# Slot one-hots of two of each four tiles made by ScalarE in the fill of the bucket lists

## What is computed

```python
edge_index = jnp.stack([src, dst])
x = _layernorm(x + _L0_gnn_ref(x, edge_index, ...), axis=-1)
x = _layernorm(x + _L1_gnn_ref(x, src, dst, ...), axis=-1)
x = _layernorm(x + _L2_gnn_ref(x, edge_index, edge_weight1, ...), axis=-1)
x = _layernorm(x + _L3_gnn_ref(x, edge_index, edge_weight, ...), axis=-1)
```

## Time and profile before

| | us |
|---|---|
| median of 3 runs | 10,757.82 |
| lowest and highest | 10,753.19, 10,758.09 |
| the profiled execution | 10,751.21 |
| its span in the trace | 10,749.4 |
| busy in the span: TensorE, VectorE | 8389.9 (78%), 8209.4 (76%) |
| busy in the span: ScalarE, GpSimd | 4510.4 (42%), 1386.4 (13%) |

### The profile page before, as it was taken

One profiled execution on the slowest core, in us unless ns is written; L12 is line 12 of the kernel. 1 busy time (PEld: TensorE's weight loads), 2 busy tenths in 40 slices (PEclk: granted clock), 3 DMA queues, 4 the chain that ended last, 5 costly groups with the idle time before them and its releaser, 6 DMA issues. The chain is left out here.

```text
span 10749.4 us, 313973 instructions
## 1 busy us (share of the span) xinstructions
PE 8389.9 (78%) x96214; PEld 6815.6 (63%) x96215; DVE 8209.4 (76%) x16705; ACT 4510.4 (42%) x9074; POOL 1386.4 (13%) x1678
## 2 busy tenths in 40 slices
PE   2244668885888755899995999798999959769996
PEld 0232225664777644899994666444999936468896
DVE  4797777777999866666666999777888777788887
ACT  0120001113666411565654444586777746423333
POOL 0110001110000000466662000000000012100000
PEclk7555555556999855999997999899999979889998
DMA  2000000001444311333331888686455400000000
GB/s 49 4 0 13 4 4 11 12 12 47 162 161 161 124 36 36 109 122 125 122 125 58 273 275 274 227 291 210 143 144 145 139 12 5 4 4 3 3 3 13
DMA packets 618663, 984.99 MB, mean 92 GB/s; under 512 B 133030, under 2 KB 278381, under 8 KB 618586
## 3 DMA queue, kind: packets, MB, share of 16 engines
q1 hardware_dynamic: 487514, 810.18, 23.8%
q10 hardware_dynamic: 121152, 162.43, 4.2%
q0 software_dynamic: 9920, 11.51, 0.4%
HBM read 788.66 MB, written 195.21 MB: 92 GB/s over the span
## 5 line engine op out<-in xcount | busy, mean ns | idle before, releaser
L2523 POOL TENSOR_TENSOR acc<-acc,m_sum 128x544 f32<-128x544 f32 (+1 forms) x637 | 810.3, 1272 | 1229.4 <-ACT m_sum L2490 1189.1
L2387 DVE TENSOR_TENSOR m_msg<-m_vps,m_msg 128x512 f32<-128x512 f32 (+1 forms) x637 | 427.3, 671 | 414.5 <-PE m_vps L2428 376.7
L2452 PE MATMUL m_sps<-m_msg,m_oh 128*128 128x136 f32 x4900 | 697.9, 286 | 0.0
L2859 PE MATMUL u_sps<-u_r,u_oh 128*128 128x129 f32 x4900 | 657.0, 276 | 28.7 <-ACT u_r L2815 28.7
L1495 PE MATMUL sp_out_x<-x,sp_adj_x 128*128 128x128 f32 x4802 | 671.6, 284 | 0.0
L1479 PE MATMUL sp_aps_x<-sp_ohw_x,sp_oh_x 128*128 128x128 bf16 x7350 | 536.6, 221 | 166.5 <-DVE sp_ohw_x L1446 166.4
L2092 PE MATMUL s_qps<-q_parts,s_oht 128*128 128x128 bf16 x7203 | 511.5, 220 | 197.9 <-DVE s_oht L1562 146.3
L1508 ACT COPY sp_adj_x<-sp_aps_x 128x512 f32<-128x512 f32 (+1 forms) x637 | 362.4, 569 | 722.6 <-PE sp_aps_x L1479 722.6
L2843 PE MATMUL u_zps<-fcs,u_a 128*128 128x128 f32 x4916 | 654.7, 276 | 6.9 <-ACT u_a L2808 6.9
L2859 PEld LDWEIGHTS u_sps<-u_r,u_oh 128*128 128x128 f32 x4900 | 598.5, 192 | 37.7 <-issue 37.6
L2452 PEld LDWEIGHTS m_sps<-m_msg,m_oh 128*128 128x128 f32 x4900 | 610.5, 191 | 0.0
(11 more groups left out here) (595 smaller groups left out, 20318.6 us busy)
## 6 DMA issues: line engine op xcount, KB each, us to landing
u_e<-e_tiles SPq DMA_DIRECT2D x591, 256.0 KB, 2.8
e_tiles<-t_es ACTq DMA_DIRECT2D x588, 256.0 KB, 4.1
g_e<-e_tiles SPq DMA_DIRECT2D x588, 256.0 KB, 4.5
s_rows<-bucket_rows SPq DMA_DIRECT2D x148, 768.0 KB, 4.0
m_rows<-bucket_rows SPq DMA_DIRECT2D x148, 768.0 KB, 4.0
t_rows<-bucket_rows SPq DMA_DIRECT2D x148, 384.0 KB, 5.0
s_rows<-bucket_rows SPq DMA_DIRECT2D x49, 896.0 KB, 5.0
m_rows<-bucket_rows SPq DMA_DIRECT2D x49, 896.0 KB, 5.0
```

Source lines behind the costliest of these rows:

```text
L2452: last = nc.tensor.matmul(sps[x][:, at:at + M], oh[x][:, j * P:(j + 1) * P], msg[x][:, j * M:(j + 1) * M], start=True, stop=True)
L2523: nc.gpsimd.tensor_tensor(at, at, sums[x][:, 0:n * M], ALU.add).then_inc(added, 1)
L2859: last = nc.tensor.matmul(sps[:, :], oh[x][:, j * P:(j + 1) * P], zr[x][:, j * D1:(j + 1) * D1], start=(q == 0 and j == 0), stop=(q == las ...
```

## The change

Of each four tiles, VectorE makes the slot one-hots of the first two only (`bf_put` shrinks from 512 to 256 columns). ScalarE makes those of the other two: for each of the two tiles a Square of (iota - slot), with the negated slot as the bias column (`bf_minus`), into `bf_far` (128 x 256, one buffer), and one Relu of (1 - `bf_far`) over both tiles into `bf_aput` (two halves). Slots are integers, so the Relu gives 1 where they agree and 0 elsewhere. ScalarE gets the inner loop and the two table reads for each window, ahead of its copy of `bf_acc`. Two semaphores are new: `bf_far_made` (ScalarE waits for its own Squares) and `bf_act_made` (Relu is done: TensorE waits for it with each group, and so does ScalarE before the next Squares). Relu also waits for `filled`. The four matmuls stay; the third and fourth read their weights from `bf_aput`. `bf_minus` is made once, at the start of the stage, by one VectorE pass over all slots.

```diff
--- before.py
+++ after.py
@@ -1262,7 +1262,9 @@
         sb, ps, sem = scope(nc, ctx, k)
         col, cur, cur_iota = sb("bf_col", 1), sb("bf_cur", NT), sb("bf_iota", s.NB)
         oht = sb("bf_oht", 2 * NT * G, BF16)
-        put, spread_ = sb("bf_put", 2 * G * P, BF16), sb("bf_spread", 2 * FQ * NT * G, BF16)
+        put, aput, far, minus = sb("bf_put", 2 * 2 * P, BF16), sb("bf_aput", 2 * 2 * P, BF16), sb("bf_far", 2 * P, BF16), sb("bf_minus", z.NGS * G)
+        spread_ = sb("bf_spread", 2 * FQ * NT * G, BF16)
+        far_made, act_made = sem("bf_far_made"), sem("bf_act_made")
         zero_b = sb("bf_zero", FQ * NT, BF16)
         acc = ps("bf_acc", FQ * NT)
         lst = sb("bf_lst", FQ * NT, BF16)
@@ -1285,7 +1287,8 @@
                 nw = B.windows(dve, s)
                 nc.vector.memset(zero_b[:, :], 0.0).then_inc(ready, 1)
                 nc.vector.tensor_copy(cur_iota[:, :], k["iota_f"][:, 0:s.NB]).then_inc(ready, 1)
-                dve.wait_ge(ready, 2)
+                nc.vector.tensor_scalar(minus[:, :], T["slot"][:, 0:z.NGS * G], -1.0, None, ALU.mult).then_inc(ready, 1)
+                dve.wait_ge(ready, 3)
                 dve.sem_inc(filled, 2)
                 with dve.Fori(0, nw) as w:
                     b, g0, g1, off = span(dve, w)
@@ -1304,7 +1307,7 @@
                                                 cur[:, :].unsqueeze(1).unsqueeze(3).broadcast_to([P, 2, NT, 2]),
                                                 T["key"][:, bass.ds(g * G, G)].rearrange("p (q t) -> p q t", t=2).unsqueeze(2)
                                                 .broadcast_to([P, 2, NT, 2]), ALU.is_equal).then_inc(tile_made, 1)
-                        pair_hot(nc, put[:, bass.ds(half * (G * P), G * P)], k["iota_2"], P, T["slot"][:, bass.ds(g * G, G)], 2)
+                        pair_hot(nc, put[:, bass.ds(half * (2 * P), 2 * P)], k["iota_2"], P, T["slot"][:, bass.ds(g * G, 2)], 1)
                         dve.wait_ge(tile_made, c + 1)
                         nc.vector.tensor_tensor(spread_[:, bass.ds(half * SP_, SP_)].rearrange("p (x v t) -> p x v t", v=NT, t=2),
                                                 here.rearrange("p (q y) -> p q y", q=2).unsqueeze(2).broadcast_to([P, 2, FQ, NT * 2]),
@@ -1323,9 +1326,11 @@
                         c = g + off
                         half = c & 1
                         pe.wait_ge(spread_made, c + 1)
+                        pe.wait_ge(act_made, c + 2)
                         for t in range(G):
+                            at = of_pair(put[:, bass.ds(half * (2 * P), 2 * P)], P, t) if t < 2 else aput[:, bass.ds(half * (2 * P) + (t - 2) * P, P)]
                             last = nc.tensor.matmul(
-                                acc[:, :], of_pair(put[:, bass.ds(half * (G * P), G * P)], P, t),
+                                acc[:, :], at,
                                 of_pair(spread_[:, bass.ds(half * SP_, SP_)], FQ * NT, t), start=False, stop=False)
                         last.then_inc(filled, 1)
                     nc.tensor.matmul(acc[:, :], zero_b[:, 0:P], zero_b[:, :], start=False, stop=True).then_inc(win_done, 1)
@@ -1334,7 +1339,19 @@
             def _(act):
                 nw = B.windows(act, s)
                 act.sem_inc(listed, 1)
+                act.sem_inc(act_made, 1)
+                act.wait_ge(ready, 3)
                 with act.Fori(0, nw) as w:
+                    b, g0, g1, off = span(act, w)
+                    with act.Fori(g0, g1) as g:
+                        c = g + off
+                        act.wait_ge(act_made, c + 1)
+                        for i in range(2):
+                            last = nc.scalar.activation(far[:, i * P:(i + 1) * P], k["iota_f"][:, :], ACT.Square, bias=minus[:, bass.ds(g * G + 2 + i, 1)])
+                        last.then_inc(far_made, 1)
+                        act.wait_ge(far_made, c + 1)
+                        act.wait_ge(filled, c + 1)
+                        nc.scalar.activation(aput[:, bass.ds((c & 1) * (2 * P), 2 * P)], far[:, :], ACT.Relu, bias=1.0, scale=-1.0).then_inc(act_made, 1)
                     act.wait_ge(win_done, w + 1)
                     act.wait_ge(stored, w * 16 + 16)
                     nc.scalar.copy(lst[:, :], acc[:, :]).then_inc(listed, 1)
```

## The result

| | before, us | after, us |
|---|---|---|
| median (4 runs each) | 10,757.95 | 10,830.44 |
| lowest and highest | 10,753.19, 10,760.07 | 10,829.40, 10,830.90 |
| span of the profiled execution | 10,749.4 | 10,829.3 |

What follows compares the result with a forecast made beforehand. A two-buffer ring of VectorE and TensorE was taken as the bound, 1.465 us a group. Terms 0 + 34 + 54 + 2 = 90 us on the 10,757.8 us median gave 10,848 us, range 10,770 to 10,925.

Steps and rivals of the forecast that it cites:

- VectorE's half one-hot: Fill stage, each group: the smaller `bf_put` saves 59 us of busy time but 0 us of elapsed time.
- The rival in which `bf_put` holds `bf_spread`: Fill stage groups: a shorter `bf_put` lets `bf_spread` start earlier, balance 26 us faster, 10,732 us; chance 0.04.
- The reading of the stage's first group: First group: a slower register instruction moved `bf_spread` to 0.65 us after `bf_oht` instead of 0.63, so `bf_put` doesn't hold it.
- The ring of two buffers: VectorE and TensorE within windows: a 2.93 us round trip carries two groups, 1.465 us each.
- ScalarE's cycle: ScalarE within windows: Squares, Relu and two waits for itself take 1.55 us a group, adding 34 us, between 0 and 96.
- TensorE's second wait: TensorE, each group: the added wait for Relu costs at most 0.05 us a group if ScalarE isn't late.
- the range above: The 0 to 96 us forecast for ScalarE's slower pace within windows.
- The crossing: Between windows: ScalarE starts the next tiles only after its copy, 4.85 us against 3.72, 54 us over 48 crossings.
- VectorE hides none of it: Between windows: VectorE's first group is ready when it was before, so it covers none of the added 1.13 us.
- Start of the stage: Ahead of the loops: one VectorE pass for `bf_minus`, which both engines wait for, 1 to 2 us once.
- Table loads: Rival: ScalarE reloads its tables in each group of the new inner loop, 563 us, 11,321 us; chance 0.01.
- ScalarE's wait for `filled`: Relu's wait until TensorE is done with the group two before, long past at this pace: 0 us.

Runs made afterwards that it cites:

- e1: Kernel before with only VectorE's one-hot halved, third and fourth tiles' matmuls reading the first two's: 10,760.28 us against 10,761.49, ratio 0.9998.
- e4: Changed kernel with VectorE making all four one-hots again, TensorE still taking the third and fourth from ScalarE: 10,832.10 us against 10,761.49 of the kernel before.
- e7: Kernel before with four buffers and VectorE's one-hot halved: 10,705.39 us, 0.9953 of the kernel before.
- e6: Kernel before with four buffers in place of two for `bf_oht`, `bf_put` and `bf_spread`: 10,701.73 us against 10,756.61, ratio 0.9949.
- e2: Kernel before with only a second, already met TensorE wait behind that for `bf_spread`: 10,803.62 us against 10,761.49, ratio 1.0038.
- e3: Changed kernel with TensorE's two waits swapped, Relu's first and `bf_spread`'s second: 10,815.71 us against 10,761.49 of the kernel before, ratio 1.0050.
- e5: Changed kernel with ScalarE reading the next window's two table values ahead of its copy: 10,791.50 us against 10,756.61 of the kernel before, ratio 1.0034.

## Why the prediction was right, and where not

The direction, the sign of each part and the range held; the time came out 18 us below the forecast, 72.5 us more than before instead of 90.

- *VectorE's half one-hot: 0.* Right, by e1, e4 and e7. The rival in which `bf_put` holds `bf_spread` is refuted three times. The reading of the stage's first group, where a slower register instruction moved `bf_spread`, was a sound sign: 24 more groups of the kernel before have that instruction at 105 ns in place of 99, and there `bf_spread` comes 633 to 637 ns after `bf_oht` in place of 627 to 631.
- *The ring of two buffers, 2.93 us.* Right: opened in e6 it gives way to VectorE's own chain, 1.33 us where 1.35 was expected.
- *ScalarE's cycle, 1.55 us, as the new bound within windows: 34 us.* This is the step that failed. The durations were nearly right (two Squares 0.69 us for 0.65, Relu 0.42 for 0.40), but the two handshakes were taken at 0.25 us each, between ScalarE's 0.20 and VectorE's 0.33, and took 0.19 and 0.14. The cycle is 1.444 us, just under the ring, and this term was 0 us in place of 34. I had named that case (0.20 each, covered by the ring) and chosen the other. I had also held a handshake of 0.14 us against the faster rival, as no row had one that short; the one over the loop's turn is that short.
- *TensorE's second wait: "one more sequencer step", at most 0.05 us a group, "inside the range above".* The size was right and the place in the sum wrong: it is what the 19 us within windows consist of (e2 and e3), and it stood in no term, since I let it count only inside the range of ScalarE's. That slower steps were forecast at all, and that their 34 us stood in for these 19, is luck: the cause was another.
- *The crossing: 4.85 us for 4.75 measured, +1.13 for +1.02, 54 us for 49.* Right in mechanism and nearly in size, by e5. ScalarE took 1.84 us from its copy to the Squares where TensorE's 1.94 had been lent to it.
- *"VectorE hides none of it: its first group is ready when it was before."* Not quite: VectorE's crossing grew by 0.27 us (3.998 for 3.726 from `bf_spread` to `bf_spread`), under ScalarE's cover.
- *Start of the stage, 2 us:* 1.5. *Table loads:* none in the new loops. *ScalarE's wait for `filled`: 0:* 1.5 us in the whole stage.
- *The Trainium skill's rates (ScalarE: Activation LUTs, What ACT_TABLE_LOAD costs):* an estimate from them is 387 ns for a Square of 128 columns and 399 for the Relu of 256, and the trace has 393 on the mean and 416. Two Squares in a row took 0.69 us, where the estimate is 0.68. The error of the sum lay in the handshakes.

What the profile was to show came mostly true: `bf_spread` 0.63 us after `bf_oht` with idle time between, crossings near 4.85, ScalarE waiting for itself. Not so the line that TensorE's wait would be put down to Relu in place of `bf_spread`: that holds for 97 of 439 groups.

## What to carry to other kernels

A busy engine is not the same as a path: an instruction that lies beside a semaphore round trip can be shortened without moving anything, and the test is whether its successor starts at its end or a fixed time after something else. It was close here: two VectorE instructions in a row overlap by 0.083 us (`bf_oht` and `bf_put`), and the `bf_put` of 0.418 us overlapped `bf_spread` by 0.074. So one longer than about 0.43 us would have held `bf_spread`; this is an estimate, and no run tried it. Before moving work to an idle engine, write down what that engine does in program order at the loop's edges, for it can only start there when its last duty, here a copy that waits for the end of the window, is done. And where an instruction gets a second wait, put the one that is met last behind the other: that was worth 0.10 us of each ring here, and two more buffers were worth more than everything that ScalarE could take over.

## What was new about the hardware

A wait that is already met, with the register arithmetic for its value, still costs TensorE's start 0.10 us when it stands behind the one that comes last (0.356 us from the end of `bf_spread` to the weight load in place of 0.260), and nothing when it stands ahead of it (0.260 in e3). And one more semaphore with one increment, executed once ahead of a loop on VectorE, made each of 48 turns of that loop 0.27 us longer (crossing 3.998 us for 3.727, 1.53 us of sequencer work for 1.28); whether the loop's place or the numbers of the semaphores does it is open.
